# Router coefficients of four units in one transpose, key-value products as 64x64 blocks, and a new order of work

## The reference, cut to what matters

```python
def _conv(x, Wq, bq, Wkv, bkv):              # on _ln_c(x): normalised over channels
    q  = einsum('nchw,oc->nohw', x, Wq) + bq
    kv = einsum('nchw,oc->nohw', x, Wkv) + bkv
    Q, K = feature(heads(q)), feature(heads(k))     # feature = elu + 1; 8 heads of 16
    den = 1 / (sum_d(Q * cumsum(K, axis=heads' length axis)) + 1e-10)
    # num: S += k v^T over the axis, o = q S (causal linear attention)
    return num * den
x = x + _conv(_ln_c(x))
t = tokens(x)                                # rows of 128 channels
def _ffn(t):                                 # on _ln_t(t)
    logits = t @ gate_w + router_gamma       # 8 experts
    combine = top-2 of softmax(logits), as an 8-wide row per token
    eo = einsum('nl,eld->end', t, expert_w) + expert_b
    return einsum('ne,end->nd', combine, gam * eo + bet)
x = from_tokens(t + _ffn(_ln_t(t)))
```

## Time and profile before

| | |
|---|---|
| median of 3 runs | 754.56 us (754.48 to 757.04) |
| the profiled execution | 755.91 us, its span 754.1 us |
| PE matmul busy | 717.1 us, 95% of the span, 8137 instructions |
| DVE busy | 685.9 us, 91%, 2550 instructions |
| ACT busy | 409.9 us, 54% |
| POOL busy | 397.8 us, 53% |
| mean granted PE clock | 0.982 of 2.4 GHz |
| DMA | 14.4% of 16 engines, 40 GB/s |

### The profile page before, as it was taken

How to read it: one execution, slowest core, us unless ns; L and a number is a source line. 1 busy time by engine, 2 the same in 40 slices (tenths; PEclk the granted TensorE clock), 3 DMA queues, 4 the chain that set the end, 5 groups by cost and what they waited for, 6 DMA issues and landing times.

```text
span 754.1 us, 23195 instructions
## 1 busy us (share of the span) xinstructions
PE 717.1 (95%) x8137; PEld 624.0 (83%) x8137; DVE 685.9 (91%) x2550; ACT 409.9 (54%) x1261; POOL 397.8 (53%) x639
## 2 busy tenths in 40 slices
PE   4767999999999999999999999999999999999986
PEld 2666888888888888888888888888888888888875
DVE  4567999999999999999999999999999999999984
ACT  1122666655555666666665555555555555555544
POOL 5145555555555555555555555555555555555520
PEclk9769999999999999999999999999999999999999
DMA  5101111111111111111111111111111111111101
GB/s 129 33 15 30 42 40 35 37 40 37 39 37 42 42 42 42 42 42 42 42 42 42 42 42 42 42 42 42 42 42 42 42 42 42 42 30 29 30 16 29
DMA packets 60214, 30.29 MB, mean 40 GB/s; under 512 B 2160, under 2 KB 60176, under 8 KB 60176
## 3 DMA queue, kind: packets, MB, share of 16 engines
q1 hardware_dynamic: 60176, 29.79, 14.4%
HBM read 20.34 MB, written 9.44 MB: 39 GB/s over the span
## 4 chain that ended last, share of the span: by engine, by line
PE 91%; DVE 4%; POOL 2%; ACT 1%; issue 1%; DMA 1%; SPq 0%; DVEq 0%; ACTq 0%; POOLq 0%
PE bank L877 11%; PE bank L915 10%; PE bank L894 9%; PE bank L916 9%; PE bank L917 9%; PE bank L933 8%; PE bank L901 4%; PE bank L909 4%; PE bank L884 4%; PE bank L853 3%; PE bank L854 3%; PE bank L855 3%; PE bank L860 3%; PE bank L847 2%; PE bank L866 2%; PE bank L935 2%
## 5 line engine op out<-in xcount | busy, mean ns | idle before, releaser
L574 DVE TENSOR_TENSOR probs<-bank,tri 128x512 f32<-128x512 f32 x288 | 184.9, 684 | 10.2 <-PE bank L877 4.7
L397 ACT ACTIVATE y_act<-bank,scale 128x128 f32<-128x128 f32 x576 | 159.4, 383 | 2.5
L915 PE MATMUL bank<-e_high,x_high 128*128 128x512 f32 x288 | 124.0, 431 | 1.1 <-DVE o L803 1.1
L916 PE MATMUL bank<-e_low,x_high 128*128 128x512 f32 x288 | 113.7, 395 | 0.0
L917 PE MATMUL bank<-e_high,x_low 128*128 128x512 f32 x288 | 113.5, 394 | 0.0
L311 POOL TENSOR_TENSOR qn<-feat,rden 128x512 f32<-128x512 f32 x36 | 38.2, 1061 | 116.4 <-DVE rden L672 116.4
L416 ACT ACTIVATE x_high<-x 128x512 fp32r<-128x512 f32 x36 | 22.8, 633 | 137.0 <-DVE x L664 137.0
L592 DVE SCALAR_TENSOR_TENSOR y_dve<-bank,scale,y_dve 128x128 f32<-128x128 f32 x288 | 92.4, 343 | 0.0
L580 DVE SCALAR_TENSOR_TENSOR qkv<-bank,rstd,b_qkv 128x384 f32<-128x384 f32 x144 | 86.8, 605 | 5.1 <-POOL rstd L301 2.6
L387 ACT ACTIVATE k_odd<-bank,parity 128x512 f32<-128x512 f32 x36 | 24.7, 687 | 114.4 <-PE bank L860 114.4
L933 PE MATMUL bank<-ident,y_act 128*128 128x128 f32 x576 | 80.8, 273 | 1.6 <-ACT y_act L397 1.6
(11 more groups left out here) (139 smaller groups left out, 1764.5 us busy)
## 6 DMA issues: line engine op xcount, KB each, us to landing
x<-in_x SPq DMA_DIRECT2D x36, 256.0 KB, 3.3
x_res<-in_x SPq DMA_DIRECT2D x36, 256.0 KB, 3.2
out<-o SPq DMA_DIRECT2D x36, 256.0 KB, 2.4
beta_raw<-in_L_ffn_beta_w SPq DMA_DIRECT2D x1, 512.0 KB
e_raw<-in_L_ffn_expert_w SPq DMA_DIRECT2D x1, 512.0 KB
w_raw<-in_L_conv_Wkv SPq DMA_DIRECT2D x2, 64.0 KB, 2.4
b_qkv<-in_L_conv_bkv SPq DMA_DIRECT2D x1, 128.0 KB, 4.4
w_raw<-in_L_conv_Wq SPq DMA_DIRECT2D x1, 64.0 KB, 2.6
```

What stands on the lines that cost most here:

```text
L397: last = nc.scalar.activation(y_act[:, p, u, e], bank[EXPERTS_AT[u][0]][:, 128 * e:128 * e + 128], ACT.Copy, scale=scale[:, p, u, e:e + 1])
L574: return tt(probs[:, half, i].rearrange("p u e t -> p (u e) t"), bank[SCORES_AT[half][i]][:].rearrange("p (n t) -> p n t", t=T), tri[:].un ...
L915: mm(out, x1_high[:, p, u], e_high[:, w], start=True, stop=False)
L916: mm(out, x1_high[:, p, u], e_low[:, w], start=False, stop=False)
```

## The change

1. *Coefficients.* coef3 becomes one block of 128 columns for all four units: for each unit, four slots of 8 (high, low, high, empty). `turn_coef` is one transpose instead of four; ACT's copy is 128x128 instead of 96x512. The bias term becomes `bias_rows`, 128 rows per unit of which only that unit's 24 are not zero, and `bias` four matmuls of 128 columns, one per unit, all with the same coef_t as the moving operand. bias_rows is made at the beginning on PE and DVE, which lengthens `rest_of_weights`.
2. *Key-value products.* `key_values` makes two 64x64 blocks per unit, each to its own 64 PSUM partitions. kv_new keeps its 128x128 layout; its off-diagonal quarters are zeroed once at the beginning, and DVE masks the two halves in two operations (`masked_blocks`) with pair_mask.
3. *Order.* LAGS is 8. The stages are now: x loaded at g[0]; turned, x_high, x_low and measured at g[2]; project and first half of the features at g[3]; second half of the features, turn_k, k_sum at g[4]; key_values, den, qn, turn_q, both halves of scores, from_state at g[5]; values, state, x1, turn_x1, logits at g[6]; experts, turn_coef, bias, turn_y, output and store at g[7]. All four engines' lists and the bank tables are new. PE's order in a step: key_values (g5); values (g6); project 3, 0 (g3); experts 00 (g7); turn_k (g4); turn_x1 (g6); experts 11; project 2, 1; experts 31, 21; turn_q (g5); turn_coef (g7); turn_x (g2); experts 30, 01; scores half 1 (g5); experts 20; bias; experts 10; turn_y 3, 0; scores half 0 (g5); from_state (g5); turn_y 2, 1. DVE's order: den, soft, hot_ab, den_eps, soft_scaled, coef, second features, scale, x1, kv_new, qkv_3, qkv_0, rden, x1 statistics, qkv_2, x1_moments, qkv_1, six y_dve, x statistics, lg0, y_dve, lg, first features, lg_max, two y_dve, lgm, probs_12, rank_a, y_dve, rank_a_max, y_dve, hot_a, x_moments, y_dve, probs_13, probs_11, lg2, probs_10, psum, lg2_max, probs_03, second, probs_00, probs_02, rank_b, probs_01, rank_b_max, out, hot_b, psum_r.

The diff, cut to its core (the engines' lists are told above):

```diff
-CONSTS = 3 + EXPERTS + 8
-FIRST_DVE = 3 + 1 + 4
-REST_DVE = 2 + 6 + EXPERTS + 2 + 4
-REST_PSUM = 2 + 6 + EXPERTS + 1
-LAGS = 6
+CONSTS = 3 + EXPERTS + 9
+FIRST_DVE = 3 + 1 + 1 + 4
+REST_COLS = 2 + 6 + EXPERTS + 1 + 1 + 2 * 4
+REST_PSUM = REST_COLS + 1
+REST_DVE = REST_PSUM + 2
+LAGS = 8
...
-AT = dict(x=4, kv=3, att=6, x1_a=6, x1_b=4, k=1, q=7, coef=0, out=1)
-PROJ_AT = (4, 0, 3, 2)
-SCORES_AT = ((3, 7, 2, 0), (0, 5, 6, 7))
-EXPERTS_AT = ((4, 2), (6, 5), (1, 1), (2, 3))
+AT = dict(x=6, kv=7, att=2, x1_a=0, x1_b=5, k=4, q=5, coef=4, out=1)
+PROJ_AT = (3, 6, 1, 1)
+SCORES_AT = ((6, 4, 0, 7), (5, 3, 2, 6))
+EXPERTS_AT = ((6, 7), (2, 2), (4, 0), (1, 3))
...
+        coef3 = sb("coef3", [128, PAR, U, QUAD // EXPERTS, EXPERTS], F32R)
+        coef_t = sb("coef_t", [128, PAR, T], F32R)
+        bias_high = sb("bias_high", [128, EXPERTS], F32R)
+        bias_cols = sb("bias_cols", [128, U, U, QUAD // EXPERTS, EXPERTS])
+        bias_rows = sb("bias_rows", [128, U, 128], F32R)
 
...
+            nc.gpsimd.memset(kv_new[:], 0.0).then_inc(S["consts"], 1)
             nc.gpsimd.memset(coef3[:].bitcast(F32), 0.0).then_inc(S["consts"], 1)
-            nc.gpsimd.memset(e_bias3[:].bitcast(F32), 0.0).then_inc(S["consts"], 1)
+            nc.gpsimd.memset(bias_cols[:], 0.0).then_inc(S["consts"], 1)
...
+                tt(pair_mask[:], heads_mask[:, 0:64], heads_mask[:, 64:128], ALU.add).then_inc(S["first_dve"], 1)
...
+                dve.wait_ge(S["rest_pe"], 4)
+                turned = bank[WEIGHTS_AT[3]][:, 0:EXPERTS]
+                make(copy(bias_high[:], turned))
+                dve.wait_ge(S["rest_dve"], done[0])
+                for u in range(U):
+                    make(copy(bias_cols[:, u, u, 0:2], bias_high[:].bitcast(F32).unsqueeze(1).broadcast_to([128, 2, EXPERTS])))
+                    make(tt(bias_cols[:, u, u, 2], turned, bias_high[:].bitcast(F32), ALU.subtract))
+                assert done[0] == REST_COLS
+                dve.wait_ge(S["rest_pe"], 5)
+                make(copy(bias_rows[:].rearrange("p u d -> p (u d)"), bank[WEIGHTS_AT[0]][:]))
...
-                for n in range(2):
-                    make(copy(e_bias3[QUAD * n:QUAD * n + EXPERTS], e_bias[:]))
-                dve.wait_ge(S["rest_dve"], done[0])
-                make(tt(e_bias3[2 * QUAD:2 * QUAD + EXPERTS], e_bias[:], e_bias3[0:EXPERTS].bitcast(F32),
-                        ALU.subtract))
...
+            def masked_blocks():
+
+                new = bank[AT["kv"]][:, 0:64 * U].rearrange("p (u d) -> p u d", u=U)
+                for i in range(2):
+                    rows = slice(64 * i, 64 * i + 64)
+                    last = tt(kv_new[rows, :, rows], new[rows],
+                              pair_mask[rows].unsqueeze(1).broadcast_to([64, U, 64]), ALU.mult)
+                return last
...
+                pe.wait_ge(S["rest_dve"], 2 + 6 + EXPERTS + 1)
+                transpose(bank[WEIGHTS_AT[3]][:, 0:EXPERTS], e_bias[:], ident[0:EXPERTS, 0:EXPERTS])\
+                    .then_inc(S["rest_pe"], 1)
+                pe.wait_ge(S["rest_dve"], REST_COLS)
+                for u in range(U):
+                    last = transpose(bank[WEIGHTS_AT[0]][:, T * u:T * u + T],
+                                     bias_cols[:, u].rearrange("p u s e -> p (u s e)"), ident[:])
+                last.then_inc(S["rest_pe"], 1)
...
                 for u in range(U):
-                    last = mm(bank[AT["kv"]][:, 128 * u:128 * u + 128], feat[:, p, u, 128:256], qkv[:, p, u, 256:384],
-                              start=True, stop=True)
-                return last
+                    for i in range(2):
+                        last = mm(bank[AT["kv"]][64 * i:64 * i + 64, 64 * u:64 * u + 64],
+                                  feat[:, p, u, 128 + 64 * i:128 + 64 * i + 64],
+                                  qkv[:, p, u, 256 + 64 * i:256 + 64 * i + 64], start=True, stop=True)
+                return last
...
+                return transpose(bank[AT["coef"]][:, 0:T], coef3[:, p].rearrange("p u s e -> p (u s e)").bitcast(F32), ident[:])
+
+            def bias(p):
+
                 for u in range(U):
-                    last = transpose(bank[AT["coef"]][0:3 * QUAD, T * u:T * u + T], coef3[:, p, u].bitcast(F32), ident[:])
-                return last
-
-            def bias(p):
-
-                return mm(bank[AT["out"]][:], e_bias3[:], coef_t[:, p], start=True, stop=False, skip_group_check=True)
+                    last = mm(bank[AT["out"]][:, T * u:T * u + T], bias_rows[:, u], coef_t[:, p], start=(u == 0),
+                              stop=False, skip_group_check=True)
+                return last
...
-                    n, p = g[2].i, g[2].par
+                    sp.dma_start(dram(out_d, p, at[7]), o[:, p]).then_inc(stored[p], 16)
+                if g[4]:
+                    n, p = g[4].i, g[4].par
                     need(sp, "x1", n - 1)
-                    sp.dma_start(x_res[:, p], dram(x_d, p, at[2])).then_inc(x_res_loaded[p], 16)
...
```

More of the change, by code:

```diff
@@ new lines, in step @@
+                if g[7]:
+                    n, p = g[7].i, g[7].par
+                    need(act, "coef_turned", n + 1)
+                    need(act, "bias", n - 1)
+                    nc.scalar.activation(coef_t[:, p], bank[AT["coef"]][:, 0:T], ACT.Copy).then_inc(S["coef_t"], 1)
+                    need(act, "experts_01", n + 1)
+                    weigh_one(p, 0).then_inc(S["y_one_0"], 1)
+                    need(act, "experts_30", n + 1)
+                    weigh_four(p, 3).then_inc(S["y_act_3"], 1)
@@ new lines, in step @@
+                if g[5]:
+                    n = g[5].i
+                    need(dve, "scores_1", n + 1)
+                    causal(1, 2).then_inc(S["probs_12"], 1)
+                if g[6]:
+                    n = g[6].i
+                    need(dve, "lgm", n + 1)
+                    stt(rank[:, 0], lgm[:], 0.0, order[:], ALU.is_ge, ALU.mult).then_inc(S["rank_a"], 1)
+                if g[7]:
+                    n, p = g[7].i, g[7].par
+                    need(dve, "y_dve_21", n + 1)
+                    weigh(p, 2, 2).then_inc(S["y_dve_22"], 1)
@@ L879, in scores @@
                 return last
-            def from_state(p):
-                for u in range(U):
-                    last = mm(bank[AT["att"]][:, T * u:T * u + T], state[:, U * p + u], q_t[:, p, u],
-                              start=(u == 0), stop=False, skip_group_check=True)
-                return last
             def values(p, half):
@@ L1051, in step @@
-                if g[3]:
-                    n = g[3].i
-                    need(pe, "qn", n + 1)
-                    turn_q().then_inc(S["q_turned"], 1)
+                        need(pe, "probs_01", n + 2)
+                        need(pe, "y_act_2", n)
+                    turn_coef(p).then_inc(S["coef_turned"], 1)
+                if g[2]:
+                    n, p = g[2].i, g[2].par
+                    pe.wait_ge(x_loaded[p], 16 * (g[2].half + 1))
+                    need(pe, "qkv_1", n)
+                    turn_x(p).then_inc(S["x_turned"], 1)
@@ new lines, in step @@
+                if g[7]:
+                    n, p = g[7].i, g[7].par
+                    need(pe, "qkv_2", n + 5)
+                    if k is not None:
+                        need(pe, "out", n)
+                    experts(p, 3, 0).then_inc(S["experts_30"], 1)
+                    need(pe, "kv_new", n + 3)
+                    if k is not None:
+                        need(pe, "probs_03", n + 2)
+                        need(pe, "y_one_0", n)
+                        need(pe, "y_dve_02", n)
+                    experts(p, 0, 1).then_inc(S["experts_01"], 1)
@@ L1066, in step @@
[L1066 to L1073 removed]
+                    need(pe, "x_parts", n + 4)
                     need(pe, "k_even", n + 1)
@@ L1076, in step @@
                     need(pe, "q_t", n + 1)
-                    need(pe, "coef_t", n - 1)
+                    need(pe, "y_dve_32", n - 1)
                     need(pe, "y_dve_12", n - 1)
+                    if k is not None:
+                        need(pe, "qkv_1", n + 3)
+                        need(pe, "y_act_0", n - 1)
+                        need(pe, "qkv_0", n + 3)
+                        need(pe, "x1", n)
+                    scores(p, 1).then_inc(S["scores_1"], 1)
+                if g[7]:
+                    n, p = g[7].i, g[7].par
+                    need(pe, "coef_t", n + 1)
+                    if k is not None:
+                        need(pe, "k_even", n + 4)
+                        need(pe, "k_odd", n + 4)
+                    experts(p, 2, 0).then_inc(S["experts_20"], 1)
+                    need(pe, "y_act_3", n + 1)
+                    if k is not None:
+                        need(pe, "qkv_2", n + 5)
+                    bias(p).then_inc(S["bias"], 1)
+                    need(pe, "probs_12", n + 3)
+                    if k is not None:
+                        need(pe, "y_one_1", n + 1)
```

(20 more changed lines are left out.)

718 lines of the change are left out of this document (324 added, 394 removed), and 15 rows, old and new, of the table names.

## The result

| | before | changed |
|---|---|---|
| median | 755.40 us (754.48 to 757.04, 4 runs) | 746.49 us (745.84 to 747.27, 4 runs) |
| the profiled execution | 755.91 us, span 754.1 | 746.64 us, span 743.9 |
| first output sum starts | 89.7 us | 101.3 us |
| one step | 19.22 us | 18.84 us |
| last five intervals between output sums | 84.3 us | 74.1 us |

The ratio is 0.9884, with a 95% interval of 0.9866 to 0.9902: 1.2% faster. The forecast was 742 us, with a range of 732 to 754. The step came out as forecast; the beginning and the end did not, with errors that largely cancel.

What follows compares the result with a forecast made beforehand. PE's instruction stream was taken to set the step: 19.22 - 0.37 = 18.85, put at 18.9 us. Span 91.7 + 30 x 18.9 + (5 x 18.9 - 15) + 3.5 = 741.7 us; median 742, range 732 to 754.

Steps and rivals of the forecast that it cites:

- What bounds the step: Whole step: PE's own instruction stream sets it, counted by the distance between starts, 19.22 us before the change.
- turn_coef: Coefficient transposes on PE: four become one at 0.109 us each, -0.33 us per step.
- bias: Bias term on PE: one 512-column matmul becomes four at 0.109 us each, +0.21 us per step, bounds 0 and +0.67.
- key_values: Key-value products on PE: 16 instructions in side-by-side pairs take 0.45 us instead of 0.90, -0.45 us per step.
- Rival (c): PE: key-value pairs serialize or bias goes at the fp32 pace; step 19.33 us, about 757 us, no change; chance 0.10.
- Changes of shape: PE's array going into and out of the new block shape ahead of values(): +0.2 us per step, bounds 0.1 and 0.35.
- the three tight places: New order: scores_0 waiting for probs_13, values(0) for four probs, DVE for proj_2; 0.05 us added to the step.
- DVE: DVE's need per step: 18.3 us plus 0.13 for the second masking operation, 18.45, leaving 0.4 of 0.9 cover.
- rival (b): DVE paces the step, with waits of 0.65 us at proj_2, turn_x and scores_1: step 19.1, 749 us; chance 0.15.
- First output: Beginning of the kernel: the first output sum starts at 91.7 us instead of 89.7, bounds 88 and 96.
- three signs of being wrong: PE waits for DVE at scores_0, bias matmuls 0.2 us apart, or a first output later than 96 us.
- Last five intervals: End of the kernel: one more partly empty step, saving 15 us against five full steps, between 11.8 and 16.

Runs made afterwards that it cites:

- pe_plus: The changed kernel with three more unused 128-column transposes per step on PE ahead of turn_coef: 758.52 us, run once.
- order_only: The changed kernel with the coefficient and key-value parts taken back, leaving the new order, lags and banks: ratio 1.0052 to the kernel before.
- dve_plus_3: The changed kernel with three more unused 128x128 DVE operations per step on SBUF operands, behind the router's last: 764.26 us, run once.
- dve_plus_1: The changed kernel with one more unused 128x128 DVE operation per step on SBUF operands, behind the router's last: 753.86 us, run once.

## Why the prediction was right, step by step

- *What bounds the step*: PE's stream, shown by pe_plus. PE busy without waits, as read from the earlier trace rows.
- *turn_coef* -0.33: it takes 0.11. Right.
- *bias* +0.21, between 0 and +0.67: 0.40 plus 0.06 at the matmul behind, instead of 0.23, so +0.23; about 0.10 for each matmul. The transpose's row was the right neighbour. The step of 18.74, the estimate from the 81 ns of the Trainium skill ("TensorE: Matmul & The Clock Gate", Back-to-back issue gap), lies 0.10 under the measured one.
- *key_values* -0.45: the pairs run side by side, 0.058 apart. The rule of the Trainium skill that spoke against it ("TensorE: Matmul & The Clock Gate", Part 3, The mechanism) does not hold in this case: all its weight loads use all rows of the array, and sixteen matmuls with the way into values() take 0.61 instead of the 0.90 they would need one by one. Rival (c) is refuted by it.
- *Changes of shape* +0.2: 0.09 ahead of key_values and 0.61 - 8 x 0.058 = 0.15 within it, less the 0.09 that values() had lost ahead of it before and does not lose a second time: +0.15. With -0.33, +0.23 and -0.44 the sum is -0.39; the step measures -0.38. The sum's 18.85 met the measured 18.84; the 0.05 added for the three tight places was not needed in the changed kernel, where PE waits at none of them. That was close: in order_only, with the same lists, the step is 0.10 longer by a wait for DVE inside turn_y, a place that the three do not include.
- *DVE* 18.3 + 0.13 = 18.45, cover 0.4: this was misread. DVE's 18.54 in the earlier trace rows already counts overlaps once, so about 18.5 was needed, not 18.3. The masking costs +0.22: its two operations take 0.83 from start to start, with 0.05 of idle time behind them, instead of 0.61. L805 costs 0.41 more, which I had not seen coming. The new order's other DVE rows are 0.4 shorter together, which hides most of it: DVE now needs 18.74 (19.32 - 0.58 in dve_plus_3), and the cover is 0.10. The forecast of the step stood by that margin, and by savings on DVE that it had not counted, which is luck; rival (b) was nearer than its chance of 0.15 says.

```profile
405.84 0.84 DVE L598 TENSOR_TENSOR kv_new<-bank,pair_mask 64x256 f32<-64x256 f32 x2
406.72 1.14 DVE L604 SCALAR_TENSOR_TENSOR qkv<-bank,rstd,b_qkv 128x384 f32<-128x384 f32 x2
```

- *First output* 91.7, bounds 88 and 96: 101.3. This step failed, beyond its bounds, and a first output later than 96 is one of the prediction's own three signs of being wrong. The term that was mis-sized is "the longer chain to scores and values costs up to 2 more, the emptier first steps give up to 2 back". Projection came at 28.1 (forecast 29) and turn_k at 38.3 (36); from turn_k to scores 17.7 instead of the 10.2 of before. I had costed the added stage as waiting within a chain, and not as one more step that has to be walked through.
- *Last five intervals* 79.5, bounds 78.5 and 82.7 (a saving of 11.8 to 16): 74.1, a saving of 20.1; the other kernels in the new order save 19.7 to 22.1. It is the same mistake with the other sign.
- *Sum*: 101.3 + 30 x 18.84 + 74.1 + 3.4 = 744.0, against 741.7 forecast. The beginning is off by +9.6, the steps by -1.8, the end by -5.4. The total was right within 0.6% in part by luck: beginning and end err in opposite directions, since a stage more makes the first output later and the last steps emptier, but that the two would largely cancel had not been worked out. Had only the beginning erred, the time would have been about 752 us, less than 3 us under the kernel before.

## What to carry to other kernels

Cost a PE edit by the distance between starts of the nearest row with the same instruction form, and blocks in different column ranges as running side by side: this gave PE's own part of each edit to 0.1 us. Put block shapes next to each other, because each stretch of them pays for its way in and out. A pipeline stage added for the order's sake is paid at the beginning with whole steps, so walk the first group through the lists before you count on it, and count one-off preparation against 36 steps of a small gain. And when two engines' lists are reordered, look which SBUF-only operations of DVE with two tensor inputs come due in the middle of long ones of POOL: here they were held to POOL's end, though the profile shows it as busy time. And do not take DVE's overlaps off twice: its busy time counts them once already, and 19.22 less 18.54 was all that it had idle.

## What the hardware showed unexpectedly

- A DVE operation of 128x32 with two SBUF inputs lasts 0.59 or 0.67 us instead of 0.18 when it comes 0.74 us behind the start of POOL's 128x512 operation of 1.3 us; in dve_plus_1 one of 128x128, 0.10 us behind the start of POOL's x_low, shows 1.32 instead of 0.25. It counts as busy, and no row of the waits names it.
- Matmuls of 64 columns in two column blocks with the same rows start in pairs every 0.058 us. In the old order their stretch costs 0.30 us beyond this pace (0.09 ahead, 0.15 within, 0.06 behind), next to values() 0.15.
- An engine that is busy throughout can still be paced by another: in order_only PE shows no idle time at turn_y, and yet a transpose there takes 0.18 instead of 0.11 in most steps, because the weight load behind it waits for DVE.
